# Loads, gate bias, a PSUM bank and the last tile: four edits to the order of an adaLN block

## The chip, the cores and the metric

One Trainium2 chip, one core. The number is the device time of one execution in microseconds. Three runs of the kernel before took 184.07, 186.6 and 189.16 us, median 186.6. The profiled execution took 184.51 us, of which the profile's span is 182.8; TensorE's granted clock was full throughout.

## The reference

Four batches (B = 4) of 512 tokens, hidden width H = 512, all in float32. A modulation vector per batch comes from `silu(c) @ wmod` in six sections (sa, ca, ga, sb, cb, gb). Then one block with one attention head of width 128, and a linear layer with four low-rank experts of rank 8, of which the gate picks one per token:

```python
mod = (_silu(L0_c) @ L0_wmod).reshape(L0_c.shape[0], 6, 1, -1)
ga = (2 * (ga >= 0) - 1) * jnp.maximum(jnp.abs(ga), 0.25)      # gb alike
h = _layernorm(x) * (1 + ca) + sa
x = x + ga * attention(h)        # q, k, v of width 128; softmax; Wo; bo
h = _layernorm(x) * (1 + cb) + sb
x = x + gb * (h @ W_up.T + lora_B[e] @ (lora_A[e] @ h))   # e = argmax(h @ gate_w.T + bias)
```

## The kernel before

Every product is made of three TensorE products of high and low parts (`products`, L391), so that each operand exists as `hi` and `lo`: ACT writes `hi` while it empties a PSUM bank, DVE subtracts it and writes `lo`. A batch is worked in these steps: layer norm 1 (DVE statistics, POOL's power, ACT or DVE normalises into `xn1`), `h1` = normalised x turned and scaled by `1 + ca`, `qkv`, scores `S`, maxima (DVE), softmax (ACT), probabilities turned (`PT`), `O`, out projection `Y`, residual and layer norm 2 (DVE, POOL, ACT), `h2`, gate and low-rank logits `gz`, their turning to tokens (`zl`, L587), the choice of the expert (DVE), `zT`, up projection `F` (four tiles of 128 tokens) closed by `lora_up` (L618), the gate product `f_gb` (DVE, L1280), the last sum (POOL, or DVE for the last two tiles, L1408), the store.

The five engines run programs written out by hand, in order, with semaphores. The programs of batch b interleave two batches: PE does batch b's attention between the pieces of batch b - 1's up projection, and then `qkv(b + 1)`. SP issues all DMAs from one queue.

In batches 0 and 1, `x` is turned by TensorE. In batches 2 and 3 (`TURNED`) it is turned in blocks of 32 by DVE (`turn_blocks`, L1148), and then 16 SBUF-to-SBUF copies on SP's queue put the blocks in place (`move_turned`, L318, from `xn` to `stage`). `h1_high` (ACT, L782) waits for all 16.

The eight PSUM banks are handed out by the table `psum_plan`: each use of a bank waits until the bank's earlier use was emptied (`open_bank`). In it, `m` are the five banks of the attention part and `f` three of the up projection. F(b - 1, 3) is in the bank of F(b - 1, 0), which is free once DVE has written `f_gb` of tile 0; on DVE this stands behind `h1_low(b + 1)`, the residual and the layer norm 2 statistics of batch b's tile 0.

`gz_evacuate` (ACT, L904) adds a bias per expert. For batch 0 this bias must be computed first: TensorE (`gate_shift_columns`), then DVE (`gate_shift`, L1118 and L1122), which in batch 1's pass stands behind `turn_blocks(2)` and `v_low`. `gate_columns("gb")` makes the second gate, TensorE turns it (`gate_to_rows`), DVE writes it to `gates`, and SP sends it to DRAM (`write_gate`, L299) and spreads it over the partitions from there.

At the start x of batch 0, the section ca, `Wqkv` and sa are issued one after the other. TensorE's `modulation(0)` needs ca; `qkv_shift_columns` (L454) needs the row of qkv's shift, which DVE adds up (`qkv_shift_row`, L1107) after the layer norm 1 of batch 1.

## Time and profile before

| | us |
|---|---|
| median of three runs | 186.6 (184.07 to 189.16) |
| profiled execution | 184.51 |
| its span | 182.8 |
| PE busy | 170.1, 93% of the span |
| DVE busy | 139.8, 76% |
| ACT busy | 90.3, 49% |
| POOL busy | 81.0, 44% |

Starts are counted from the beginning of the span. An engine's idle time stands in square brackets behind the instruction that ended it, with what released it. Starts of consecutive matmuls tell their pace; their own durations overlap.

### The profile page before, as it was taken

How to read it: one execution, taken by the hardware profiler on the slowest of the kernel's cores; microseconds unless marked ns; L12 is line 12 of the kernel's file. 1: busy time of each engine (PE TensorE's matmuls, PEld its weight loads, DVE VectorE, ACT ScalarE, POOL GpSimd, SP SyncE). 2: the span in 40 equal slices, each digit the busy share in tenths (PEclk: the TensorE clock that was granted, in tenths of full speed). 3: DMA queues.
4: the chain of work that ended last, by engine and by line, in shares of the span. 5: the costliest groups of instructions: out<-in, count | busy, mean ns of one | idle time of the engine just before them, and what ended most of it. 6: DMA issues, size and time to landing. Idle time of an engine off the chain costs nothing.

```text
span 182.8 us, 2810 instructions
## 1 busy us (share of the span) xinstructions
PE 170.1 (93%) x911; PEld 133.6 (73%) x911; DVE 139.8 (76%) x350; ACT 90.3 (49%) x170; POOL 81.0 (44%) x109
## 2 busy tenths in 40 slices
PE   6778999999999959998999999999999999999990
PEld 6654756978678738786888787868887878768870
DVE  1837859997969999869997919699288294988964
ACT  3356145964268874176438552713396512484100
POOL 3464200279335984008769830018695000362650
PEclk9999999999999999999999999999999999999999
DMA  4999995930051014440023741001140000001414
GB/s 155 381 385 387 390 383 98 375 120 11 0 166 69 2 26 105 102 170 6 32 83 136 190 107 31 0 0 57 61 152 24 0 2 0 0 0 61 172 43 186
DMA packets 13758, 21.32 MB, mean 117 GB/s; under 512 B 3324, under 2 KB 3840, under 8 KB 13744
## 3 DMA queue, kind: packets, MB, share of 16 engines
q1 hardware_dynamic: 13744, 21.15, 34.3%
q8 instruction: 7, 0.11, 0.3%
q14 instruction: 7, 0.06, 0.1%
HBM read 14.83 MB, written 4.21 MB: 104 GB/s over the span
## 4 chain that ended last, share of the span: by engine, by line
PE 65%; DVE 18%; ACT 6%; DMA 4%; issue 4%; SPq 1%; POOL 0%; DVEq 0%; ACTq 0%; POOLq 0%
PE bank L391 43%; DMA stage<-in_L_wmod_dram 4%; PE bank L405 3%; DVE h1lo L1137 3%; PE bank L515 3%; DVE xs L1215 2%; DVE stats L1222 2%; PE bank L542 2%; DVE row_max L1189 2%; ACT xn_p L830 2%; DVE f_gb L1280 2%; DVE h2lo L1153 1%; DVE xn L1148 1%; PE bank L494 1%; PE bank L500 1%
## 5 line engine op out<-in xcount | busy, mean ns | idle before, releaser
L391 PE MATMUL bank<-wup_lo,h2hi 128*128 128x512 f32 x64 | 26.8, 418 | 1.3 <-DVE f_gb L1280 0.9
L1466 POOL TENSOR_TENSOR rstd<-var_eps,neg_half 128x1 f32<-128x1 f32 x16 | 8.8, 553 | 41.4 <-DVE var_eps L1226 41.4
L869 ACT ACTIVATE xn_p<-xs,shift,rstd 128x512 f32<-128x512 f32 x16 | 13.1, 817 | 25.9 <-POOL shift L1469 25.9
L391 PE MATMUL bank<-wup_hi,h2hi 128*128 128x512 f32 x64 | 25.3, 395 | 0.0
L391 PE MATMUL bank<-wup_hi,h2lo 128*128 128x512 f32 x64 | 25.2, 394 | 0.0
L1481 POOL TENSOR_TENSOR xs<-xs,f_gb 128x512 f32<-128x512 f32 x14 | 17.9, 1294 | 7.7 <-DVE f_gb L1280 7.7
L391 PE MATMUL bank<-h1lo,wqkv_hi 128*128 128x512 f32 x48 | 19.7, 410 | 0.8 <-DVE modT_ca L1057 0.8
L1458 POOL TENSOR_TENSOR xs<-xs,gabo 128x512 f32<-128x512 f32 x16 | 20.2, 1293 | 0.1
L391 PE MATMUL bank<-h1hi,wqkv_hi 128*128 128x512 f32 x48 | 19.0, 395 | 0.0
L391 PE MATMUL bank<-h1hi,wqkv_lo 128*128 128x512 f32 x48 | 18.9, 394 | 0.0
L391 PEld LDWEIGHTS bank<-wup_lo,h2hi 128*128 128x128 f32 x64 | 12.0, 188 | 4.5 <-DVE f_gb L1280 1.8
L1198 DVE TENSOR_TENSOR plo<-bank,phi 128x512 fp32r<-128x512 f32 x16 | 10.0, 684 | 6.8 <-ACT phi L838 6.7
L391 PEld LDWEIGHTS bank<-wup_hi,h2hi 128*128 128x128 f32 x64 | 12.0, 188 | 2.8
L1215 DVE SCALAR_TENSOR_TENSOR xs<-bank,row_inv,xs 128x512 f32<-128x512 f32 x16 | 12.0, 748 | 2.2 <-PE bank L391 1.3
L391 PEld LDWEIGHTS bank<-wup_hi,h2lo 128*128 128x128 f32 x64 | 12.1, 189 | 2.0
L830 ACT ACTIVATE xn_p<-bank,neg_max 128x512 f32<-128x512 f32 x16 | 11.0, 687 | 4.9 <-DVE neg_max L1191 4.9
L1003 DVE BATCH_NORM_STATS2 stats<-xs 128x6 f32<-128x512 f32 x16 | 10.2, 679 | 3.4 <-DMA xs<-in_L_attn_x_dram 3.4
L391 PEld LDWEIGHTS bank<-h1lo,wqkv_hi 128*128 128x128 f32 x48 | 9.0, 188 | 4.2 <-issue 2.4
L1443 POOL TENSOR_TENSOR wo_ga<-wo_raw,ga_bc 128x512 f32<-128x512 f32 x4 | 5.6, 1396 | 14.1 <-DMA ga_bc<-gates_dram 10.9
L1280 DVE TENSOR_TENSOR f_gb<-bank,gb_bc 128x512 f32<-128x512 f32 x16 | 10.6, 687 | 1.6 <-PE bank L618 1.5
L1222 DVE BATCH_NORM_STATS2 stats<-xs 128x6 f32<-128x512 f32 x16 | 11.1, 695 | 0.8
L838 ACT ACTIVATE phi<-bank 128x512 fp32r<-128x512 f32 x16 | 8.4, 606 | 6.0 <-PE bank L515 6.0
(181 smaller groups left out, 414.5 us busy)
## 6 DMA issues: line engine op xcount, KB each, us to landing
out_dram<-xs SPq DMA_DIRECT2D x16, 256.0 KB, 2.0
...
xs<-in_L_wmod_dram SPq DMA_DIRECT2D x3, 1024.0 KB, 10.1
...
stage<-xn SPq DMA_DIRECT2D x32, 64.0 KB, 2.0
...
gb_bc<-gates_dram SPq DMA_DIRECT2D x4, 256.0 KB, 3.7
```

Source lines behind the costliest of these rows:

```text
L391: mm = nc.tensor.matmul(dst, w, m, start=first and i == 0, stop=last and i == total - 1)
L830: nc.scalar.activation(xn2_p[:, t, :], at("S", b, t)[:], ACT.Exp, bias=neg_max[:, t:t + 1], scale=SCORE_SCALE, accum_out=row_sum[:, t:t + ...
L838: nc.scalar.activation(phi[:, :, t * P:(t + 1) * P], at("PT", b, t)[:].rearrange("p (k q) -> p k q", k=NT), ACT.Copy).then_inc(S["pt_hi"], 1)
L869: nc.scalar.activation(xn2_p[:, t, :], xs[:, b, t, :], ACT.Identity, bias=shift[:, 1, t:t + 1], scale=rstd[:, 1, t:t + 1]).then_inc(S["xn2 ...
L1003: nc.vector.bn_stats(stats[:, 0, t, :], xs[:, b, t, :]).then_inc(S["ln1_stats"], 1)
L1198: nc.vector.tensor_tensor(plo[:, :, q], at("PT", b, t)[:].rearrange("p (k q) -> p k q", k=NT), phi[:, :, q].bitcast(F32), ALU.subtract).th ...
L1215: nc.vector.scalar_tensor_tensor(xs[:, b, t, :], at("Y", b, t)[:], row_inv[:, t:t + 1], xs[:, b, t, :], ALU.mult, ALU.add).then_inc(S["x2_ ...
L1222: nc.vector.bn_stats(stats[:, 1, t, :], xs[:, b, t, :]).then_inc(S["ln2_stats"], 1)
L1280: nc.vector.tensor_tensor(f_gb[:, n % 4, :], at("F", b, t)[:], gb_bc[:, b % 2, :], ALU.mult).then_inc(S["f_gb_ready"], 1)
L1458: nc.gpsimd.tensor_tensor(xs[:, b, t, :], xs[:, b, t, :], gabo[:], ALU.add).then_inc(S["xb_ready"], 1)
L1466: nc.gpsimd.tensor_tensor(rstd[:, 1, t:t + 1], var_eps[:, 1, t:t + 1], neg_half[:, 0:1], ALU.pow).then_inc(S["ln2_rstd"], 1)
L1481: nc.gpsimd.tensor_tensor(xs[:, b, t, :], xs[:, b, t, :], f_gb[:, n % 4, :], ALU.add).then_inc(S["out_ready"], 1)
```

## The change

Four things are edited.

1. **Loads.** x of batch 0 comes in three loads (tile 0, tile 1, tiles 2 and 3). SP issues the first half of `Wqkv` only when tile 1 is in, and section sa only when all of x is in. DVE normalises tile 3 of x before it writes the first modulation rows, and TensorE turns tile 3 before the modulation columns.
2. **Gate bias.** In batch 1's pass, DVE does `gate_shift` and `gate_columns("gb")` right behind the maxima, `turn_blocks(2)` behind `v_low`, and the statistics of batch 3 behind `o_low`. ACT does `wo_high(1)` and two of the four normalisations of batch 2 after `gz_evacuate(0)`. SP puts the write of the second gate between the first eight and the last eight copies of turned blocks.
3. **Bank.** F(b - 1, 3) of batches 0 and 1 is in the bank of zT(b - 1), and qkv(b + 1)'s first output in the bank of F(b - 1, 0).
4. **Last tile.** The last tile of the last batch is computed in two halves of 256 columns, each in a bank of its own, with a multiply, an add and a store of its own, and `z_transposes` of the second half stands before it.

```diff
@@ -77,15 +77,15 @@
...
         order += [(m[4], "zT", b - 1), (f[2], "F", b - 1, 2)]
-        order += [(m[i], "Y", b, t) for t, i in enumerate((1, 2, 3, 0))] + [(f[0], "F", b - 1, 3)]
+        order += [(m[i], "Y", b, t) for t, i in enumerate((1, 2, 3, 0))] + [(f[0] if last else m[4], "F", b - 1, 3)]
         if not last:
-            order += [(m[i], "qkv", b + 1, j) for j, i in enumerate((4, 1, 2))]
+            order += [(f[0], "qkv", b + 1, 0), (m[1], "qkv", b + 1, 1), (m[2], "qkv", b + 1, 2)]
             order += [(m[3], "x2T", b, 0), (m[0], "x2T", b, 1), (f[1], "x2T", b, 2), (f[2], "x2T", b, 3)]
-            m, f = (f[0], m[4], m[1], m[2], m[3]), (m[0], f[1], f[2])
+            m, f = (m[4], f[0], m[1], m[2], m[3]), (m[0], f[1], f[2])
         else:
...
                       (m[0], "x2T", b, 3), (m[1], "gz", b, 0), (m[4], "F", b, 1), (m[3], "zl", b, 0), (m[1], "gz", b, 1),
-                      (f[0], "zl", b, 1), (f[1], "F", b, 2), (m[0], "zT", b, 0), (f[2], "F", b, 3), (m[1], "zT", b, 1)]
+                      (f[0], "zl", b, 1), (f[1], "F", b, 2), (m[0], "zT", b, 0), (m[1], "zT", b, 1), (f[2], "side", 0), (m[3], "side", 1)]
     place, earlier, holds = {}, {}, [None] * 8
...
@@ -196,7 +196,7 @@
...
         wqkv_in = [sem(f"wqkv_in{kt}") for kt in range(NK)]
-        x0_in = [sem(f"x0_in{i}") for i in range(2)]
+        x0_in = [sem(f"x0_in{i}") for i in range(3)]
         x_in = [sem(f"x_in{b}") for b in range(B)]
...
@@ -264,6 +264,9 @@
...
 
+        def columns_of(side):
+            return slice(side * H // 2, (side + 1) * H // 2)
+
         def xn1_done(engine, b, t=NT):
...
@@ -297,9 +300,9 @@
...
                 sp.dma_start(gates_dram[i], gates[:, i, :]).then_inc(gates_out, 16)
+
+            def spread_gate(i, b):
                 sp.wait_ge(gates_out, 16 * (i + 1))
-
-            def spread_gate(i, b):
                 if b >= 2 and i == 0:
...
@@ -308,22 +311,25 @@
...
 
-            def move_turned(b):
-
-                sp.wait_ge(S["xn1_turned"], NT * (b - TURNED + 1))
-                if b > TURNED:
-                    sp.wait_ge(S["h1_lo"], NK * b)
-                for a in range(NB):
+            def move_turned(b, blocks=range(NB)):
+
+                if blocks[0] == 0:
+                    sp.wait_ge(S["xn1_turned"], NT * (b - TURNED + 1))
+                    if b > TURNED:
+                        sp.wait_ge(S["h1_lo"], NK * b)
+                for a in blocks:
                     for c in range(NB):
...
             sp.dma_start(c_rows[0:B, :], c).then_inc(c_in, 16)
-            for i in range(2):
-                sp.dma_start(xs[:, 0, 2 * i:2 * i + 2], x_v[0, :, 2 * i:2 * i + 2, :]).then_inc(x0_in[i], 16)
+            for i, ts in enumerate((slice(0, 1), slice(1, 2), slice(2, 4))):
+                sp.dma_start(xs[:, 0, ts], x_v[0, :, ts, :]).then_inc(x0_in[i], 16)
             load_section("ca")
+            sp.wait_ge(x0_in[1], 16)
             load_wqkv((0, 1))
+            sp.wait_ge(x0_in[2], 16)
             load_section("sa")
...
@@ -351,8 +357,9 @@
...
             sp.dma_start(xs[:, 3], x_v[3]).then_inc(x_in[3], 16)
-            move_turned(2)
+            move_turned(2, (0, 1))
             write_gate(1)
+            move_turned(2, (2, 3))
             spread_gate(1, 0)
...
@@ -360,15 +367,17 @@
...
                     move_turned(3)
-                for t in range(NT):
-                    if b == LAST and t >= 2:
-                        sp.wait_ge(last_out_ready, t - 1)
-                    else:
-                        sp.wait_ge(S["out_ready"], NT * b + t + 1)
+                for t in range(NT if b < LAST else 2):
+                    sp.wait_ge(S["out_ready"], NT * b + t + 1)
                     sp.dma_start(out_v[b, :, t, :], xs[:, b, t, :]).then_inc(stored, 16)
...
                     spread_gate(1, b + 2)
-            sp.wait_ge(stored, 16 * B * NT)
+            sp.wait_ge(last_out_ready, 1)
+            sp.dma_start(out_v[LAST, :, 2, :], xs[:, LAST, 2, :]).then_inc(stored, 16)
+            for side in range(2):
+                sp.wait_ge(last_out_ready, 2 + side)
+                sp.dma_start(out_v[LAST, :, 3, columns_of(side)], xs[:, LAST, 3, columns_of(side)]).then_inc(stored, 16)
+            sp.wait_ge(stored, 16 * (B * NT + 1))
 
...
@@ -618,6 +627,16 @@
...
 
+            def last_tile_side(side, kts):
+
+                q, n = slice((NT - 1) * P, T), columns_of(side)
+                whole = open_bank("side", side) if kts[0] == 0 else at("side", side)
+                dst = whole[:, n]
+                products(dst, [((h2hi[:, kt, q], h2lo[:, kt, q]), (wup_hi[:, kt, n], wup_lo[:, kt, n])) for kt in kts],
+                         first=kts[0] == 0, last=False)
+                if kts[-1] == NK - 1:
+                    nc.tensor.matmul(dst, zT[:, q], lbw[:, n], start=False, stop=True).then_inc(S["F_psum"], 1)
+
             def gate_transposes():
...
@@ -679,9 +698,9 @@
...
             first_x1_transposes((2,))
+            first_x1_transposes((3,))
             first_modulation_columns(0)
             first_modulation_columns(1)
-            first_x1_transposes((3,))
             keep_warm(bank[5], 3)
...
@@ -764,12 +783,12 @@
...
             lora_up(b, 1)
-            up(b, 3, (0, 1))
             z_transposes(b, 1)
-            up(b, 3, (2,))
+            for side in range(2):
+                last_tile_side(side, (0, 1, 2))
             lora_up(b, 2)
-            up(b, 3, (3,))
-            lora_up(b, 3)
+            for side in range(2):
+                last_tile_side(side, (3,))
 
...
@@ -845,8 +864,8 @@
...
 
-            def ln1_normalise(b):
-                for t in range(NT):
+            def ln1_normalise(b, tiles=range(NT)):
+                for t in tiles:
                     act.wait_ge(S["ln1_shift"], BY_ACT + NT * (b - 2) + t + 1)
...
@@ -955,14 +974,16 @@
...
             h2_high(0)
-            wo_high(1)
-            ln1_normalise(2)
+            ln1_normalise(2, (0, 1))
             for b in range(1, B):
...
                 gz_evacuate(b - 1)
+                if b == 1:
+                    wo_high(1)
+                    ln1_normalise(2, (2, 3))
                 pt_high(b)
...
@@ -996,7 +1017,7 @@
...
                     if b == 0:
-                        dve.wait_ge(x0_in[t // 2], 16)
+                        dve.wait_ge(x0_in[min(t, 2)], 16)
                     else:
...
@@ -1310,8 +1331,8 @@
...
                 first_ln1_variance(t)
+            first_ln1_normalise()
             first_modulation_rows()
-            first_ln1_normalise()
             first_columns(0)
...
@@ -1357,14 +1378,11 @@
...
                 if b == 1:
-                    turn_blocks(2)
+                    gate_shift()
+                    gate_columns("gb")
                 v_low(b)
                 if b == 1:
-                    gate_shift()
-                    ln1_stats(3, (0, 1, 2, 3))
-                    ln1_moments(3)
-                if b == 1:
-                    gate_columns("gb")
+                    turn_blocks(2)
                 pt_low(b)
...
@@ -1372,6 +1390,8 @@
...
                 if b == 1:
+                    ln1_stats(3, (0, 1, 2, 3))
+                    ln1_moments(3)
                     ffn_shift_rows()
...
@@ -1401,11 +1421,20 @@
...
             gate_ffn(LAST, 1)
-            for t in (2, 3):
-                gate_ffn(LAST, t)
-                n = NT * LAST + t
-                dve.wait_ge(S["f_gb_ready"], n + 1)
-                nc.vector.tensor_tensor(xs[:, LAST, t, :], xs[:, LAST, t, :], f_gb[:, n % 4, :],
+            gate_ffn(LAST, 2)
+            n = NT * B - 2
+            dve.wait_ge(S["f_gb_ready"], n + 1)
+            nc.vector.tensor_tensor(xs[:, LAST, 2, :], xs[:, LAST, 2, :], f_gb[:, n % 4, :],
+                                    ALU.add).then_inc(last_out_ready, 1)
+            n = NT * B - 1
+            dve.wait_ge(S["out_ready"], n - 3)
+            for side in range(2):
+                part = columns_of(side)
+                dve.wait_ge(S["F_psum"], n + side + 1)
+                nc.vector.tensor_tensor(f_gb[:, n % 4, part], at("side", side)[:, part], gb_bc[:, LAST % 2, part],
+                                        ALU.mult).then_inc(S["f_gb_ready"], 1)
+                dve.wait_ge(S["f_gb_ready"], n + side + 1)
+                nc.vector.tensor_tensor(xs[:, LAST, 3, part], xs[:, LAST, 3, part], f_gb[:, n % 4, part],
                                         ALU.add).then_inc(last_out_ready, 1)
...
```

**DVE, batch 1's pass, behind the scores.** Before, behind the last `neg_max`; `gz_sum` and `gz_bias` the gate bias, `stats<-xs` the statistics of batch 3:

```order
L1148 STREAM_TRANSPOSE xn<-xn 128x16x32 x4
L1182 TENSOR_TENSOR v_lo<-bank,v_hi 128x512
L1118 TENSOR_REDUCE gz_sum<-bank 72x4
L1122 TENSOR_SCALAR gz_bias<-gz_sum,eb_col 72x4
L1003 BN_STATS stats<-xs 128x6 x4
L1008 BN_AGGR moments<-stats 128x2 x4
L1010 TENSOR_SCALAR var_eps<-moments 128x4
L1088 SCALAR_TENSOR_TENSOR gate_tmp<-mod_sum 128x16
L1090 TENSOR_SCALAR gate_tmp<-mod_sum 128x16
L1093 TENSOR_SCALAR gate_tmp<-gate_tmp 128x16
L1096 SCALAR_TENSOR_TENSOR gate_col<-gate_tmp 128x16
L1198 TENSOR_TENSOR plo<-bank,phi 128x4x128 x4
```

Now:

```order
L1212 TENSOR_SCALAR neg_max<-row_max 128x1
L1139 TENSOR_REDUCE gz_sum<-bank 72x4
L1143 TENSOR_SCALAR gz_bias<-gz_sum,eb_col 72x4
L1109 SCALAR_TENSOR_TENSOR gate_tmp<-mod_sum 128x16
L1111 TENSOR_SCALAR gate_tmp<-mod_sum 128x16
L1114 TENSOR_SCALAR gate_tmp<-gate_tmp 128x16
L1117 SCALAR_TENSOR_TENSOR gate_col<-gate_tmp 128x16
L1203 TENSOR_TENSOR v_lo<-bank,v_hi 128x512
L1169 STREAM_TRANSPOSE xn<-xn 128x16x32 x4
L1219 TENSOR_TENSOR plo<-bank,phi 128x4x128 x4
L1123 COPY gates<-bank 4x512
```

The bias and the second gate moved ahead of `v_lo`, the block turns behind it, and the statistics out of the piece.

**ACT, the same place.** Before; `xn_p,row_sum` is the softmax, `xn<-xs` the normalisation of batch 2:

```order
L880 ACTIVATE h2hi<-bank,modT_cb 128x512 x4
L895 ACTIVATE wo_hi<-wo_ga 128x512
L856 ACTIVATE xn<-xs,shift,rstd 128x4x4x32 x4
L830 ACTIVATE xn_p,row_sum<-bank,neg_max 128x512 x3
L819 ACTIVATE v_hi<-bank 128x512
L830 ACTIVATE xn_p,row_sum<-bank,neg_max 128x512
L904 ACTIVATE gz<-bank,gz_bias 72x512
L838 ACTIVATE phi<-bank 128x4x128 x4
```

Now:

```order
L899 ACTIVATE h2hi<-bank,modT_cb 128x512 x4
L875 ACTIVATE xn<-xs,shift,rstd 128x4x4x32 x2
L849 ACTIVATE xn_p,row_sum<-bank,neg_max 128x512 x3
L838 ACTIVATE v_hi<-bank 128x512
L849 ACTIVATE xn_p,row_sum<-bank,neg_max 128x512
L923 ACTIVATE gz<-bank,gz_bias 72x512
L914 ACTIVATE wo_hi<-wo_ga 128x512
L875 ACTIVATE xn<-xs,shift,rstd 128x4x4x32 x2
L857 ACTIVATE phi<-bank 128x4x128 x4
```

`wo_hi` and two of the four normalisations stand behind `gz`, the softmax comes two normalisations and a `wo_hi` sooner.

**SP, the copies of turned blocks and what follows.** Before:

```order
L353 DMA xs<-in_L_attn_x_dram 128x4x512
L318 DMA stage<-xn 32x512 x16
L299 DMA gates_dram<-gates 4x512
L309 DMA gb_bc<-gates_dram 128x512 x2
L309 DMA ga_bc<-gates_dram 128x512
L368 DMA out_dram<-xs 128x512 x4
```

Now:

```order
L359 DMA xs<-in_L_attn_x_dram 128x4x512
L322 DMA stage<-xn 32x512 x8
L302 DMA gates_dram<-gates 4x512
L322 DMA stage<-xn 32x512 x8
L312 DMA gb_bc<-gates_dram 128x512 x2
L312 DMA ga_bc<-gates_dram 128x512
L372 DMA out_dram<-xs 128x512 x4
```

The write of the gates stands between two groups of eight copies; the spreads of both gates stay behind all of them.

## Rows read from the trace of the kernel before

**Rows 1.** The page: busy time by engine; transfer rate in 40 slices of 4.6 us.
```profile
PE 170.1 (93%) x911; PEld 133.6 (73%) x911; DVE 139.8 (76%) x350; ACT 90.3 (49%) x170; POOL 81.0 (44%) x109
...
GB/s 155 381 385 387 390 383 98 375 120 11 0 166 69 2 26 105 102 170 6 32 83 136 190 107 31 0 0 57 61 152 24 0 2 0 0 0 61 172 43 186
```

**Rows 2.** Timeline of PE (start us, us, engine, line, tiles, idle before, releaser).
```profile
68.76 0.44 PE L587 MATMUL bank<-ident,gz 72*128 72x72 f32 x4 [2.27 <-ACT gz L904]
...
86.11 0.50 PE L391 MATMUL bank<-wup_lo,h2hi 128*128 128x512 f32 x1 [0.58 <-DVE f_gb L1280]
...
122.16 0.50 PE L391 MATMUL bank<-wup_lo,h2hi 128*128 128x512 f32 x1 [0.34 <-DVE f_gb L1280]
```

**Rows 3.** Chain of waits, in order of time (start us, us, what).
```profile
2.19 7.96 DMA stage<-in_L_wmod_dram
...
89.40 8.36 PE bank L391 x36
```

**Rows 4.** Timeline of DVE and PE, 17 to 25 us.
```profile
17.69 2.47 DVE L1003 BATCH_NORM_STATS2 stats<-xs 128x6 f32<-128x512 f32 x4 [0.35 <-DMA xs<-in_L_attn_x_dram]
...
23.83 0.56 DVE L1107 TENSOR_TENSOR qb_row<-bank,bqkv_rows 128x384 f32<-128x384 f32 x1
...
24.53 0.52 PE L454 MATMUL bank<-ident,qb_row 128*128 128x128 f32 x3
```

**Rows 5.** View of tile xs, batch 1's x load, issued at 5.8.
```profile
DMA to landing us min/median/max: 11.9/11.9/11.9
```

**Rows 6.** Timeline of ACT and DVE, 60 to 68 us.
```profile
60.88 2.92 ACT L856 ACTIVATE xn<-xs,shift,rstd 128x512 f32<-128x512 f32 x4
...
63.81 0.15 DVE L1191 TENSOR_SCALAR neg_max<-row_max 128x1 f32<-128x1 f32 x1
...
67.11 0.72 DVE L1122 TENSOR_SCALAR gz_bias<-gz_sum,eb_col 72x4 f32<-72x4 f32 x1
```

**Rows 7.** Timeline of ACT, DVE and PE, 79 to 108 us.
```profile
79.97 2.55 ACT L782 ACTIVATE h1hi<-stage,modT_ca 128x512 fp32r<-128x512 f32 x4
...
85.36 0.69 DVE L1280 TENSOR_TENSOR f_gb<-bank,gb_bc 128x512 f32<-128x512 f32 x1
...
93.16 2.48 DVE L1148 STREAM_TRANSPOSE xn<-xn 128x512 f32<-128x512 f32 x4
...
97.13 1.13 DVE L1172 SCALAR_TENSOR_TENSOR qk_lo<-bank,qb,qk_hi 128x128 fp32r<-128x128 f32 x4 [1.49 <-ACT qk_hi L808]
...
99.10 2.73 DVE L1153 SCALAR_TENSOR_TENSOR h2lo<-bank,modT_cb,h2hi 128x512 fp32r<-128x512 f32 x4 [0.19 <-ACT h2hi L880]
...
106.04 0.69 ACT L904 ACTIVATE gz<-bank,gz_bias 72x512 f32<-72x512 f32 x1
...
107.19 0.41 PE L587 MATMUL bank<-ident,gz 72*128 72x72 f32 x4
```

**Rows 8.** Timeline of SP's issues, 66 to 77 us.
```profile
66.39 10.10 SPq L318 DMA_DIRECT2D stage<-xn  x16
...
76.54 0.48 SPq L299 DMA_DIRECT2D gates_dram<-gates  x1
```

**Rows 9.** The page, DMA issues (count, KB each, us to landing).
```profile
out_dram<-xs SPq DMA_DIRECT2D x16, 256.0 KB, 2.0
...
stage<-xn SPq DMA_DIRECT2D x32, 64.0 KB, 2.0
```

**Rows 10.** Timeline, operations of 256 columns, and DVE's last add.
```profile
11.33 0.76 DVE L1049 TENSOR_SCALAR gb_bc<-bank 128x256 f32<-128x256 f32 x2 [1.89 <-PE bank L405]
...
169.00 0.28 PE L578 MATMUL bank<-h2hi,gzw 128*72 128x256 f32 x1
...
169.12 0.28 PE L579 MATMUL bank<-h2lo,gzw 128*72 128x256 f32 x1
...
179.61 0.69 DVE L1408 TENSOR_TENSOR xs<-xs,f_gb 128x512 f32<-128x512 f32 x1
```

**Rows 11.** The page, costliest groups (busy us, mean ns, idle before).
```profile
L391 PEld LDWEIGHTS bank<-wup_hi,h2hi 128*128 128x128 f32 x64 | 12.0, 188 | 2.8
```

## The prediction, before the changed kernel ran

> **What bounds the kernel now.** I read the page first, then the chain of waits, then the timeline around each idle stretch of PE. TensorE is busy 93% of the span [rows 1], so only time in which it stands still, and the two ends of the kernel, can be given back. Behind the start its larger stops are three [rows 2]: 2.27 us before batch 0's expert logits are turned (L587), and 0.58 and 0.34 us before the fourth up projection of batches 0 and 1, which finds its bank still held by the first. The start hangs on `ca`: issued at 2.19, in 7.96 us later, at 10.15 [rows 3]. Around it the loads run at 381 to 390 GB/s [rows 1]. The tail is DVE's multiply and add of the last tile, then a store.
>
> **Part 1, loads held back.** The bytes ahead of `ca`'s last one (x 1.05 MB, `ca` 1.05 MB) take 5.4 us at 390 GB/s, and they flow from about 2.8, so `ca` could be in at 8.2 plus the time to be reported, against 10.15: at most some 1.3 us are lost to loads behind it. The nearest evidence on whether they are: the queue was never empty, and x of batch 1, issued behind everything, landed 11.9 us after its issue [rows 5]. That is time in a full queue, not the transfer's own. [...]
>
> More important is who uses such a gain. If PE starts qkv earlier it arrives earlier at L454, the turning of the shift row. That row comes from DVE, at 23.83 + 0.56 = 24.39, and PE takes it at 24.53 [rows 4]. DVE's work between runs without a break of note from x of batch 1, which DVE waited for until 17.69 (ln1 statistics, POOL's power, four normalisations, the shift row) [rows 4]. PE's slack there is 0.1 us. So whatever `ca` gains is handed back at L454 unless x of batch 1 also lands earlier, and that load moves behind two waits. Moving the modulation rows behind tile 3's normalisation, and PE's columns behind tile 3's transposes, costs at most the 0.2 us of four transposes, and is absorbed at the same place. Bounds -1.3 and +2.4 (the latter below, as a rival); I take **0**, since the row nearest to it, L454, has no slack.
>
> **Part 2, gate bias ahead.** PE's 2.27 us wait ends with ACT's `gz`, and this with DVE's `gz_bias`, which starts at 67.11 [rows 6] behind four block turns and v_low. Now it stands right behind the last negated maximum (63.96), so it is ready at about 64.9. ACT no longer normalises four tiles first (2.92 us from 60.88 [rows 6]); two of them and wo_high come behind `gz`. Its softmaxes then follow DVE's maxima, and `gz` is done at about 65.7, before PE needs it at 66.3. The whole stop goes: **-2.27** on PE. The work put aside must still be done. ACT after 63.96: softmax, `gz` and wo_high at 0.7 each (a `gz` takes 0.69 [rows 7]), two normalisations at 0.73: about 67.6. DVE's last of four turns, 0.62 of 2.48 [rows 7], ends near 68.4, where all four ended at 66.39 before. pt_low starts there, in time for pv at 71.6. Statistics of batch 3 (2.5 us) move behind o_low into a stretch in which DVE then waits for ACT's h1; I cost them at nothing, and if that cover went, 2.5 us would fall on h1_low.
>
> The copies of turned blocks do not hide. The 16 issues take 10.10 us on SP [rows 8], the last lands 2.0 us after its issue [rows 9]. They start 2.0 later, and between the eighth and the ninth stands the write of the gates, 0.48 us [rows 8] (its data is there at 72.2, before the eighth issue ends). The last copy was in at 77.9 and now is at 80.4. ACT began batch 2's h1 at 79.97 [rows 7], so h1 and all that DVE has queued behind it come **0.5 later** than before, while PE is 2.27 earlier.
>
> **Part 3, the bank.** F(0,3) now follows zT(0), which is emptied 6 us earlier, so the 0.58 disappears where it stood; PE could be at the end of up(0,3) at 89.40 - 2.27 - 0.58 = 86.55 (89.40 is where qkv(2) began [rows 3]). But qkv(2) has now the bank of F(0,0), so the wait for the same evacuation moves there: 85.36 + 0.69 [rows 7] + 0.5 = 86.55. By luck the two meet; qkv(2) starts about 2.8 earlier.
>
> **Where part of it is given back.** Scores of batch 2 need qk_lo. DVE's second set of turns ended at 93.16 + 2.48 = 95.64 and qk_lo started at 97.13, having waited for ACT, which waited for PE [rows 7]. With PE 2.8 earlier and DVE 0.5 later, qk_lo is bound by DVE's queue: it starts at 96.2, only 0.95 earlier. h2_low, which stood behind it with a small wait (0.19), comes 1.1 earlier, and so do the maxima and softmaxes. ACT's `gz` moves from 106.04 to 104.95 and ends at 105.65; PE, which was at L587 at 107.19 [rows 7] without a wait, waits now until then. Left: **-1.55**. In batch 2 the bank change takes 0.34 away [rows 2]; there h1 waited for PE and not for copies, so nothing is late: **-0.34**. From there all engines keep step with PE.
>
> **Part 4, the last tile in halves.** 24 matmuls of 256 columns stand for 12 of 512. The nearest rows, logits in halves, follow each other at 0.12 us [rows 10], 24 of them as long as 12 at 0.23: 0. If each instead took the 188 ns of a full weight load [rows 11], PE would be 24 x 0.07 = 1.7 later. I take 0, since in the rows with 256 columns the load was hidden. DVE then does two multiplies and two adds of half size. A half-size operation took 0.38 (0.76 for two), a whole one 0.69 [rows 10], so four against two are 0.14 more, partly overlapped: **+0.1**. DVE was the last to finish (179.61 + 0.69). The last store has half the bytes, but 64 KB copies and 256 KB stores both land in 2.0 [rows 9]: 0. The end gains nothing, which is the opposite of what the edit suggests.
>
> **Sum:** 0 - 1.55 - 0.34 + 0.1 = -1.8 us. The profiled execution took 184.51 (span 182.8), which gives 182.7. The three runs are 184.07, 186.6 and 189.16; with the profiled one their median is 1.05 above it. I add that much: **183.7**.
>
> **Rivals.**
> - *The start pays too (B).* x of batch 1 lands earlier with `ca`, and the 1.3 us pass L454: 181.4. For it: `ca` was 1.3 us later than its bytes. Against it: queue full before and after, L454 without slack.
> - *The copies eat it (C).* SP takes the gate write late, or batch 3's copies, which start half a microsecond later too, hold ACT, or the statistics put off push h1_low: 1 to 2 us more for DVE's queue behind 80.4, and every microsecond of it goes through qk_lo to PE: about 184. For it: 10.10 us of issues for one pass. Against it: DVE has 2 us of idle time before h1_low.
> - *Slower (D): the held loads come late.* x of batch 1 was issued at 5.8 and is now issued behind two waits, at about 8.2. Should its 11.9 us from issue to landing [rows 5] be its own time, it lands 2.4 later, at 20.1, and DVE's chain from 17.69 to 24.39 moves by 2.4, with PE at L454 behind it. Slower than before from a delay of 1.8 us on; at 2.4: 182.7 + 2.4 = 185.1. Against it: full bandwidth until then [rows 1], so its bytes should not be later.
> - *The bank change does nothing*: partly in the forecast already, since in batch 1 the wait only moves from up(0,3) to qkv(2); it costs or saves 0.6 at most.
>
> **Chances.** Forecast 0.52, B 0.23, C 0.15, D 0.10. The forecast's own range is 1.2 to 2.9 us of gain. Over the cases the sums reach from 181.4 to 185.1; the medians of runs can lie from 0.6 below to 1.9 above such a sum: 180.8 to 187.0. A measurement of this kernel can tell about 2%, 3.7 us. The forecast is 1% and B 1.7%; only with halves of B, or all bounds on the good side, or runs of before that all fall high, is it over 2% faster: 0.27. Slower by over 2% takes D and more: 0.06. Within: 0.67.
>
> **What would show it.** L587 of batch 0 without idle time, at about 66.3. SP's first copies at 68.4, the gate write between eight and eight, ACT's first `h1hi<-stage` at 80.4 rather than 79.97. No wait of PE before up(0,3); one for `f_gb` before qkv(2), or none. qk_lo of batch 2 straight behind the block turns, and a short wait of PE at scores and at L587 of batch 1. `ca` at 9 to 10 and PE at L454 still at 24.4 to 24.6: if it is at 23.2, B is right; at 26 or later, D. At the end, DVE's last add 0.1 later behind PE's last matmul than before. The forecast is wrong if the start moves L454, if a weight load shows between the half-size matmuls, or if copies take longer than 10.1 us to issue.

## The result and the profile after

| | before | after |
|---|---|---|
| median of 11 runs, us | 184.51 (183.73 to 189.21) | 182.92 (181.78 to 183.54) |
| profiled execution | 184.51 | 182.96 |
| its span | 182.8 | 181.2 |
| PE busy | 170.1 (93%) | 170.8 (94%) |

The ratio is 0.9923, 95% interval 0.9894 to 0.9951: faster by 0.8%, less than the 2% called a difference. Runs of the kernel before (and, below, of e10) fall in two groups, here six around 184 (median 184.03) and four around 189, with one at 186.6 between them, of which the ratios use the lower one alone; none of the changed kernel's runs lay near 189.

First the page of the changed kernel, to be held against [rows 1]; slices of 4.53 us.

```profile
PE 170.8 (94%) x924; PEld 134.9 (74%) x924; DVE 139.6 (77%) x352; ACT 90.1 (50%) x170; POOL 80.4 (44%) x109
...
GB/s 130 313 352 379 387 385 234 269 206 52 0 54 183 0 0 50 98 109 157 0 114 33 213 139 83 0 0 56 65 149 26 0 2 0 0 4 58 174 41 190
```

The loads are slower at the start: over the first four slices 1174 GB/s summed against 1308 before, which over 4.55 us each is 0.61 MB not yet moved. Profiles of the experiments below bear this out: the four kernels in which SP waits between loads have sums of 1174 to 1266, the ten others 1268 to 1320.

Timeline of PE: its stops from 8 us on that a bracket names, and four places without one (lines are shifted: L596 is L587 of before, L463 is L454, L400 is L391). Two more stops are not shown, since the kernel before has them too: 0.26 us at 38.27 (before 0.26 at 37.48) and 0.38 at 161.53 (before 0.37 at 163.00).

```profile
10.59 1.07 PE L414 MATMUL bank<-stage,silu_wide 128*32 128x512 f32 x8 [2.24 <-DMA stage<-in_L_wmod_dram]
15.61 0.47 PE L400 MATMUL bank<-h1lo,wqkv_hi 128*128 128x512 f32 x1 [1.17 <-ACT wqkv_hi L881]
25.32 0.52 PE L463 MATMUL bank<-ident,qb_row 128*128 128x128 f32 x3
...
67.12 0.41 PE L596 MATMUL bank<-ident,gz 72*128 72x72 f32 x4
87.54 0.47 PE L400 MATMUL bank<-h1lo,wqkv_hi 128*128 128x512 f32 x1 [0.40 <-DVE f_gb L1301]
98.69 0.50 PE L509 MATMUL bank<-qk_lo,qk_hi 128*128 128x512 f32 x1 [0.15 <-DVE qk_lo L1197]
106.31 0.44 PE L596 MATMUL bank<-ident,gz 72*128 72x72 f32 x4
...
132.21 1.91 PE L551 MATMUL bank<-ident,xn_p 128*128 128x128 f32 x16
```

Of the stops in [rows 2] none is left where it stood. In exchange there are 0.40 us before batch 2's qkv and 0.15 before its scores, and the start is late: L454 was reached at 24.53 [rows 4], now at 25.32.

Timeline of DVE, ACT and SP, the pieces that answer to [rows 4], [rows 6], [rows 7] and [rows 8].

```profile
18.41 2.47 DVE L1024 BATCH_NORM_STATS2 stats<-xs 128x6 f32<-128x512 f32 x4 [0.39 <-DMA xs<-in_L_attn_x_dram]
...
24.62 0.56 DVE L1128 TENSOR_TENSOR qb_row<-bank,bqkv_rows 128x384 f32<-128x384 f32 x1 [0.21 <-PE bank L455]
...
64.89 0.23 DVE L1143 TENSOR_SCALAR gz_bias<-gz_sum,eb_col 72x4 f32<-72x4 f32 x1
65.86 0.68 ACT L923 ACTIVATE gz<-bank,gz_bias 72x512 f32<-72x512 f32 x1
...
69.24 5.04 SPq L322 DMA_DIRECT2D stage<-xn  x8
74.33 0.48 SPq L302 DMA_DIRECT2D gates_dram<-gates  x1
74.85 4.94 SPq L322 DMA_DIRECT2D stage<-xn  x8
...
81.30 2.56 ACT L801 ACTIVATE h1hi<-stage,modT_ca 128x512 fp32r<-128x512 f32 x4 [2.88 <-DMA stage<-xn]
86.70 0.69 DVE L1301 TENSOR_TENSOR f_gb<-bank,gb_bc 128x512 f32<-128x512 f32 x1
94.49 2.48 DVE L1169 STREAM_TRANSPOSE xn<-xn 128x512 f32<-128x512 f32 x4
96.90 1.08 DVE L1193 SCALAR_TENSOR_TENSOR qk_lo<-bank,qb,qk_hi 128x128 fp32r<-128x128 f32 x4
```

`gz_bias` starts at 64.89, `gz` at 65.86, and PE finds it done at 67.12. Then the new chain. The view of the chain of waits of the changed kernel, 67 to 87 us, shows it (start, us, what):

```profile
67.80 1.43 DVE xn L1169 x2
69.24 0.61 SPq L322
...
79.20 2.02 DMA stage<-xn
81.30 0.73 ACT h1hi L801
82.05 1.90 DVE h1lo L1158 x3
```

The program's end now goes through SP: block turns, seventeen issues one behind the other, the landing of the last copy, h1, DVE's queue, and from there to PE. On the page, SP's issues are 6% of the chain that ended last, and were 1% before.

### The profile page after: what moved, and what is told of

The parts are those of the page before. It is cut to its first block, busy times and chain, and to the rows that moved or that the text cites. A ratio compares the mean times of both kernels' runs of the same rounds, so it can differ in the third digit from the quotient of the medians.

```text
span 181.2 us, 2841 instructions
## 1 busy us (share of the span) xinstructions
PE 170.8 (94%) x924; PEld 134.9 (74%) x924; DVE 139.6 (77%) x352; ACT 90.1 (50%) x170; POOL 80.4 (44%) x109
## 4 chain that ended last, share of the span: by engine, by line
PE 57%; DVE 18%; ACT 8%; SPq 6%; DMA 6%; issue 4%; POOL 0%; DVEq 0%; ACTq 0%; POOLq 0%
PE bank L400 37%; SPq L322 5%; DMA stage<-in_L_wmod_dram 4%; PE bank L414 3%; DVE xs L1236 3%; ACT xn_p L849 3%; DVE stats L1243 3%; DVE xn L1169 2%; PE bank L524 2%; DVE f_gb L1301 1%; DVE h1lo L1158 1%; DVE h2lo L1174 1%; PE bank L509 1%; PE bank L503 1%; DMA stage<-xn 1%
## 5 line engine op out<-in xcount | busy, mean ns | idle before, releaser
L400 PE MATMUL bank<-wup_lo,h2hi 128*128 128x512 f32 (+1 forms) x68 | 27.2, 401 | 0.4 <-ACT h2hi L907 0.4
L400 PE MATMUL bank<-wup_hi,h2hi 128*128 128x512 f32 (+1 forms) x68 | 26.0, 382 | 0.0
L400 PE MATMUL bank<-wup_hi,h2lo 128*128 128x512 f32 (+1 forms) x68 | 25.9, 381 | 0.0
L400 PE MATMUL bank<-h1lo,wqkv_hi 128*128 128x512 f32 x48 | 19.7, 411 | 1.6 <-ACT wqkv_hi L881 1.2
L1487 POOL TENSOR_TENSOR xs<-xs,gabo 128x512 f32<-128x512 f32 x16 | 20.3, 1308 | 0.1
L400 PE MATMUL bank<-h1hi,wqkv_hi 128*128 128x512 f32 x48 | 19.0, 395 | 0.0
L400 PE MATMUL bank<-h1hi,wqkv_lo 128*128 128x512 f32 x48 | 18.9, 394 | 0.0
L400 PEld LDWEIGHTS bank<-wup_lo,h2hi 128*128 128x128 f32 x68 | 12.8, 188 | 2.7 <-issue 0.6
L400 PEld LDWEIGHTS bank<-wup_hi,h2hi 128*128 128x128 f32 x68 | 12.8, 188 | 2.6
L400 PEld LDWEIGHTS bank<-wup_hi,h2lo 128*128 128x128 f32 x68 | 12.9, 189 | 1.9
L400 PEld LDWEIGHTS bank<-h1lo,wqkv_hi 128*128 128x128 f32 x48 | 9.0, 188 | 5.4 <-issue 2.3
L1301 DVE TENSOR_TENSOR f_gb<-bank,gb_bc 128x512 f32<-128x512 f32 x15 | 9.9, 685 | 1.7 <-PE bank L627 1.5
L1210 DVE TENSOR_REDUCE row_max<-bank 128x1 f32<-128x512 f32 x16 | 10.9, 681 | 0.1
L400 PEld LDWEIGHTS bank<-h1hi,wqkv_hi 128*128 128x128 f32 x48 | 9.0, 188 | 2.2
```

Source lines behind the costliest of these rows:

```text
L400: mm = nc.tensor.matmul(dst, w, m, start=first and i == 0, stop=last and i == total - 1)
L1210: nc.vector.reduce_max(row_max[:, t:t + 1], at("S", b, t)[:], AX_X).then_inc(S["max_ready"], 1)
L1301: nc.vector.tensor_tensor(f_gb[:, n % 4, :], at("F", b, t)[:], gb_bc[:, b % 2, :], ALU.mult).then_inc(S["f_gb_ready"], 1)
L1487: nc.gpsimd.tensor_tensor(xs[:, b, t, :], xs[:, b, t, :], gabo[:], ALU.add).then_inc(S["xb_ready"], 1)
```

## The experiments

Unless a time is called a span, it is a median of runs. Spans are those of the profiled executions; ratios are to runs of the kernel before on the same chip. The experiments ran in three groups, each on a chip of its own: e1, e2, e3 and e5; e6 to e9; e4, e10, e11 and e12. Medians are compared safely within a group only; across groups the ratios are to be compared, with their intervals. "Old start" means part 1 undone.

**e1: part 1 undone, everything else as changed.**

```diff
-            for i, ts in enumerate((slice(0, 1), slice(1, 2), slice(2, 4))):
-                sp.dma_start(xs[:, 0, ts], x_v[0, :, ts, :]).then_inc(x0_in[i], 16)
+            for i in range(2):
+                sp.dma_start(xs[:, 0, 2 * i:2 * i + 2], x_v[0, :, 2 * i:2 * i + 2, :]).then_inc(x0_in[i], 16)
             load_section("ca")
-            sp.wait_ge(x0_in[1], 16)
             load_wqkv((0, 1))
-            sp.wait_ge(x0_in[2], 16)
...
-            first_ln1_normalise()
             first_modulation_rows()
+            first_ln1_normalise()
```

> The changed kernel with its start as before: x in two loads, nothing held back, the modulation rows and columns in their old order. The other three parts stay. My theory (the held loads cost time): in the changed kernel ca is in at 10.55 instead of 10.15 and PE is at L454's turning at 25.45 instead of 24.53, so undoing the start gives 0.9 us back: ca at 10.15, L454 at 24.5, the first turned logits about 65.5, qkv(2) at 86.7, span 180.3, ratio to the kernel before 0.987. Rival (the difference at the start is spread between executions of one and the same program, or is swallowed later where DVE and SP bind): the span stays at 181.2, ratio 0.992.

Measured: 182.16 (181.69 to 182.78), ratio 0.9886 [0.9853, 0.9919], span 180.3. Timeline of DVE and PE of e1:

```profile
16.87 2.46 DVE L1022 BATCH_NORM_STATS2 stats<-xs 128x6 f32<-128x512 f32 x4
...
24.26 0.52 PE L461 MATMUL bank<-ident,qb_row 128*128 128x128 f32 x3
```

DVE takes x of batch 1 at 16.87, not 18.41, and PE is at the shift row 1.06 us before the changed kernel. The span is shorter by 0.9 us. The intervals of the two ratios overlap, so e1 alone does not prove that part 1 costs; e10, and e11 against e12, do. Which piece of it costs, the next four ask.

**e2, e3, e4, e10: the pieces of part 1.** e2 keeps the three loads and the new order and drops SP's two waits. e3 keeps the waits and the order, with x in two loads. e4 keeps the order alone. e10 is the kernel before with part 1 alone.

```diff
 e2, against the changed kernel
-            sp.wait_ge(x0_in[1], 16)
...
-            sp.wait_ge(x0_in[2], 16)
 e3, against the changed kernel
-            for i, ts in enumerate((slice(0, 1), slice(1, 2), slice(2, 4))):
+            for i in range(2):
...
-            sp.wait_ge(x0_in[1], 16)
+            sp.wait_ge(x0_in[0], 16)
             load_wqkv((0, 1))
-            sp.wait_ge(x0_in[2], 16)
+            sp.wait_ge(x0_in[1], 16)
```

> The changed kernel without the two waits in SP's queue: x still in three loads, new order on DVE and PE. If the waits starve the transfer engines (313 GB/s in the second fortieth of the span against 381 before), this one has 380 there, all of x in by 6.3, ca at 10.2 to 10.5 (its issue stays 0.4 later), L454 at 24.6 to 24.9. If the smaller first loads are what slows the transfers, the rate stays near 313, all of x is in at 7.9 and L454 stays at 25.4.

> The changed kernel with x in two loads as before, but with the waits: the first half of Wqkv is issued when the first half of x is in, section sa when all of it is. If the waits starve the transfers: rate near 313 in the second fortieth, second half of x later than 6.1, ca at 10.2 or later, L454 near 25.1. If the split in three is the cause: rate 380, ca earlier than 10.15, L454 at 24.5.

> The changed kernel with the loads of before (two loads of x, no waits on SP's queue), but the new order on DVE (tile 3 normalised before the first modulation rows) and on TensorE (tile 3 turned before the modulation columns). Theory: the order alone costs at most 0.3 us, since the work only changes places ahead of the same landing of x of batch 1; PE at L454 at 24.2 to 24.6, time as with the whole start of before, 182.2. Rival: the order is what costs, 0.5 us or more, PE at L454 at 24.9 or later with x of batch 1 landing at 17.5 or before.

> The kernel before with part 1 alone: x of batch 0 in three loads, the two waits on SP's queue, and the new order of DVE and TensorE at the start. Theory (the start costs, because held loads arrive later): PE reaches the turning of the shift row (L454) at 25.1 to 25.4 instead of 24.1 to 24.6, x of batch 1 lands at about 18.4, and since the rest is the order of before, with its 2.27 us stop at L587 that waits for ACT and DVE, which are late by the same 0.8, all of it passes on: 0.7 to 0.9 us slower than before, span about 183.6. Rival (the start is neutral, and the 0.8 us between the changed kernel and the one with the old start was the spread between executions): no difference, ratio 1.000. Rival of the prediction (start pays): 1 us faster.

Starts in the profiled executions (us), and medians:

| | x loads | waits | order | `ca` issued | PE takes `ca` | to qkv(0) | DVE takes x of batch 1 | L454 | median | ratio |
|---|---|---|---|---|---|---|---|---|---|---|
| before | 2 | no | old | 2.19 | 10.20 | +4.62 | 17.69 | 24.53 | 184.51 | 1 |
| e8 | 2 | no | old | 2.19 | 10.30 | +4.62 | 17.81 | 24.63 | | |
| e1 | 2 | no | old | 2.19 | 9.32 | +5.23 | 16.87 | 24.26 | 182.16 | 0.9886 [0.9853, 0.9919] |
| e4 | 2 | no | new | 2.19 | 9.46 | +5.03 | 17.01 | 24.20 | 182.09 | 0.9888 [0.9867, 0.9909] |
| e2 | 3 | no | new | 2.57 | 9.99 | +5.03 | 17.51 | 24.73 | 182.49 | 0.9895 [0.9865, 0.9925] |
| e3 | 2 | yes | new | 2.19 | 10.39 | +5.02 | 17.87 | 25.12 | 181.96 | 0.9863 [0.9816, 0.9911] |
| after | 3 | yes | new | 2.57 | 10.59 | +5.02 | 18.41 | 25.32 | 182.92 | 0.9923 [0.9894, 0.9951] |
| e11 | 3 | yes | new | 2.56 | 10.17 | +5.03 | 18.64 | 25.26 | 181.59 | (another edit, below) |

The ratios of e1 to e4 can't be told apart: their intervals overlap, and e3, with the waits, has the lowest. So the medians don't say which piece costs, and what follows on the pieces is read from starts in single profiles.

e10, part 1 alone on the kernel before, has the ratio 1.0044 [1.0022, 1.0067]: 0.8 us slower. Its interval leaves out no change, and gain as well. It rests on three of its nine runs (184.68 to 185.25), and the median of all nine is 190.3. In its profiled execution, span 190.7, TensorE's clock fell behind `ca` (last section), so it is not in the table.

One regularity reads the table: in twelve of the thirteen profiles with the clock at full level there, PE reaches L454 9.70 to 9.72 us after it starts qkv(0). No bracket names a wait on the way, so what is late at qkv(0) is late at L454. Only in e11 does it wait there, 0.22 us for DVE's row, behind the latest x of batch 1, at 18.64. So DVE's row and PE run nearly level, and elsewhere PE's own work sets when it arrives.

From before to after that gives +0.39 for `ca` and +0.40 for what lies between `ca` and qkv(0). In this pair of traces the first is an issue: the third load of x puts `ca` on the queue at 2.57 instead of 2.19, and it lands in 7.98 us against 7.96. From one profile to the next the landing varies more than that, from 6.8 to 8.1 us without waits, so the pair can't show it by itself. The second is the order. Timeline of PE of e9 (old order, described below), then of e4 (new order), which both take `ca` at the same time:

```profile
9.44 1.07 PE L412 MATMUL bank<-stage,silu_wide 128*32 128x512 f32 x8 [0.59 <-DMA stage<-in_L_wmod_dram]
...
11.16 0.60 PE L469 MATMUL bank<-ident,xn 128*128 128x128 f32 x4
11.59 0.60 PE L420 MATMUL bank<-ident,gb_bc 128*128 128x128 f32 x4
...
14.26 0.47 PE L398 MATMUL bank<-h1lo,wqkv_hi 128*128 128x512 f32 x1 [0.77 <-ACT wqkv_hi L879]
```

```profile
9.46 1.06 PE L412 MATMUL bank<-stage,silu_wide 128*32 128x512 f32 x8 [0.48 <-DMA stage<-in_L_wmod_dram]
...
11.17 1.04 PE L469 MATMUL bank<-ident,xn 128*128 128x128 f32 x8
12.05 0.60 PE L420 MATMUL bank<-ident,gb_bc 128*128 128x128 f32 x4
...
14.49 0.47 PE L398 MATMUL bank<-h1lo,wqkv_hi 128*128 128x512 f32 x1 [1.17 <-ACT wqkv_hi L879]
```

Tile 3's four transposes (L469, eight in a row instead of four) take 0.44 us ahead of the columns (L420), and the columns make `modT_ca`, without which no h1 is. With `ca` at 9.45 this costs 0.2 at qkv(0), where the old order is not bound by the columns: tile 3's transposes then wait for DVE to normalise it (in e1, with `ca` at 9.32, PE waits 0.41 us for that, and the distance is even +5.23). With `ca` later than 9.8 the old order's distance is 4.62 to 4.65 in five profiles and the new one's 5.02, the whole 0.4. e4's median does not show it.

Last the waits. SP's issues of e1 and of the changed kernel tell what they do. First e1:

```profile
2.70 0.99 SPq L294 DMA_DIRECT2D xn_p<-in_L_attn_Wqkv_dram  x2
...
5.66 0.38 SPq L335 DMA_DIRECT2D xs<-in_L_attn_x_dram  x1
```

and the changed kernel:

```profile
4.55 1.07 SPq L294 DMA_DIRECT2D xn_p<-in_L_attn_Wqkv_dram  x2
...
9.72 0.41 SPq L337 DMA_DIRECT2D xs<-in_L_attn_x_dram  x1
```

x of batch 1 (L337) is issued 4.06 us later than in e1 and used 1.54 later: most of its time was queue, but not all. And `ca`, for which the others stood back, gained nothing: PE took it at 10.17 to 10.84 in the four profiles with waits (e10's included), at 9.05 to 10.30 in the ten without, and from issue to landing it took 7.6 to 8.2 us with waits, 6.8 to 8.1 without. That the waits make it later is likely but not shown, since those ranges overlap and e3's median is no worse than e1's; that they don't bring it forward is.

**e5: the last tile whole, old start.**

```diff
-            for side in range(2):
-                last_tile_side(side, (0, 1, 2))
+            up(b, 3, (0, 1))
+            z_transposes(b, 1)
+            up(b, 3, (2,))
             lora_up(b, 2)
-            for side in range(2):
-                last_tile_side(side, (3,))
+            up(b, 3, (3,))
+            lora_up(b, 3)
```

> Start as before and the last tile whole as before; gate bias and bank as in the changed kernel. In the changed kernel DVE's last add ended 0.27 us later behind the gate product of tile 2 than before (3.01 against 2.74), but the span ended 2.1 us behind that add against 2.5. My theory: the halves cost DVE 0.27 and the half-size store gives 0.4 back, so this kernel is 0.1 us slower than e1_old_start, not to be told apart by its time; from the tile-2 gate product to the end of the span 5.2 us here, 5.1 in e1. Rival (as forecast: the store gives nothing): 0.1 to 0.3 us faster than e1_old_start.

Measured: 182.13 (181.75 to 182.31), ratio 0.9882 [0.9861, 0.9903], span 180.5; e1 182.16. Timeline of DVE at the end, e1 first, then e5:

```profile
175.15 0.69 DVE L1299 TENSOR_TENSOR f_gb<-bank,gb_bc 128x512 f32<-128x512 f32 x1 [1.54 <-PE bank L625]
...
177.73 0.42 DVE L1435 TENSOR_TENSOR xs<-xs,f_gb 128x256 f32<-128x256 f32 x1
```

```profile
175.28 0.69 DVE L1297 TENSOR_TENSOR f_gb<-bank,gb_bc 128x512 f32<-128x512 f32 x1 [1.52 <-PE bank L623]
...
177.33 0.69 DVE L1424 TENSOR_TENSOR xs<-xs,f_gb 128x512 f32<-128x512 f32 x1
```

From tile 2's product to the last add's end it is 3.00 us with halves and 2.74 whole; from there to the span's end 2.15 and 2.48. DVE loses 0.26, and 0.33 comes back behind its last add, where the last store has half the size. Part 4 is worth nothing either way.

**e6: the gate write behind all sixteen copies, old start.**

```diff
-            move_turned(2, (0, 1))
-            write_gate(1)
-            move_turned(2, (2, 3))
+            move_turned(2)
+            write_gate(1)
```

> Start as before; gate bias, bank and halves as in the changed kernel, but SP writes the second gate behind all 16 copies instead of between eight and eight. If the issue of the copies is what binds batch 2's h1 (ACT started it at 80.31 in e1_old_start, released by the last copy), the last copy and h1 come 0.5 earlier (79.8), the gate product of tile 0 too (85.2), and qkv(2) starts at 86.1 instead of 86.55; 0.4 us less in the span: 179.9. The gate spreads land about 1 us later, which I expect to be hidden. Rival (POOL's output weights, which wait for the spread, bind layer norm 2): h1 0.5 earlier, but nothing gained or up to 0.5 lost by the scores of batch 2.

Measured: 182.85 (181.88 to 183.34), ratio 0.9868 [0.976, 0.9976], span 181.3: not the gain of 0.4 that was expected. The copies took 10.34 us instead of 10.52 with the write between them (e1), and ACT's h1 began 11.86 us behind their start instead of 12.06. Against these 0.2 us the spreads of the gates started 1.5 later on SP (80.32 against 78.83), since they wait for the write to land. The way from there to PE can be read in the two traces: POOL, which multiplies the output weights by the spread gate (`wo_ga`), starts that at 86.35 instead of 84.80, POOL's powers for layer norm 2 stand behind it in its queue, and ACT's first `xn_p` of batch 1's layer norm 2, which needs them, starts at 89.80 instead of 88.25. ACT's last is late too, and PE stops where e1 had no stop. Timeline of PE of e6:

```profile
95.79 1.97 PE L548 MATMUL bank<-ident,xn_p 128*128 128x128 f32 x16 [0.75 <-ACT xn_p L885]
```

By these traces the place of the write is right: between the copies it costs 0.2 us, behind them some 0.8 us of span (1.0, of which 0.2 stood already at L454, 24.44 against 24.26). The ratios of e6 and e1 don't tell them apart.

**e7: the bank table as before, all other parts but the start changed. e8: the kernel before with the new bank table alone.**

```diff
 e7, against the changed kernel (besides the old start)
-        order += [...] + [(f[0] if last else m[4], "F", b - 1, 3)]
+        order += [...] + [(f[0], "F", b - 1, 3)]
...
-            m, f = (m[4], f[0], m[1], m[2], m[3]), (m[0], f[1], f[2])
+            m, f = (f[0], m[4], m[1], m[2], m[3]), (m[0], f[1], f[2])
 e8, against the kernel before: the same lines the other way round
```

> Start as before, gate bias and halves as in the changed kernel, the bank plan as before: F(0,3) again behind F(0,0). My theory: the two parts are worth something only together, because the DVE queue is 0.3 to 0.5 later and PE waits there: up(0,3) starts only at 86.5 with 3.5 us of idle time before it, qkv(2) at 89.8, scores at 99.9, in batch 2 another 0.4; the span 182.8 to 183.3, no better than the kernel before, ratio 0.997 to 1.003. Rival (the gains add up one by one): 1.0 to 1.3 us slower than e1_old_start, span 181.5, ratio 0.994.

> The kernel before with the new bank plan alone. My theory: here the DVE queue keeps its old times, qkv(2) may start at once behind up(0,3), so both stops go: 0.7 in batch 1's pass and 0.5 in batch 2's, span 181.6, ratio 0.9935. Rival (the wait only moves to qkv(2), which now shares the bank of F(0,0)): qkv(2) where it was at 89.3, span 182.3 or more, ratio 0.998.

e7: 186.07 (184.63 to 187.54; 186.00 over the five runs that the ratio uses), ratio 1.0032 [0.9937, 1.0128], span 184.4. e8: 184.95 (182.55 to 187.3; 183.93 over the four that the ratio uses), ratio 0.9932 [0.9792, 1.0072], span 181.5. Timeline of PE of e7, the fourth up projection of batch 0 and what follows:

```profile
82.52 0.40 PE L625 MATMUL bank<-lbw,zT 128*128 128x512 f32 x1
86.23 0.65 PE L398 MATMUL bank<-wup_lo,h2hi 128*128 128x512 f32 x1 [3.31 <-DVE f_gb L1299]
...
87.11 0.63 PE L398 MATMUL bank<-wup_hi,h2hi 128*128 128x512 f32 x1
87.54 0.63 PE L398 MATMUL bank<-wup_lo,h2hi 128*128 128x512 f32 x1
...
90.22 0.39 PE L398 MATMUL bank<-wup_hi,h2lo 128*128 128x512 f32 x1
90.46 0.39 PE L398 MATMUL bank<-wup_hi,h2hi 128*128 128x512 f32 x1
```

and PE's busy time by windows there (window, length, busy, granted clock, DMA share, GB/s):

```profile
86.00:88.00 2.00, 1.77 (x5) 0.61 0.00 0
88.00:90.00 2.00, 2.00 (x7) 0.54 0.00 0
90.00:92.00 2.00, 2.00 (x10) 1.00 0.34 131
```

Without the new bank the time that PE gains at L587 is lost in front of the fourth up projection, which finds its bank held until DVE's `f_gb` at 85.49: the stop there grows from 0.58 to 3.31 us. Behind it the granted clock is at its lower level, 1.2 GHz: eight matmuls follow each other at 0.42 to 0.43 us instead of 0.235, another 1.5 us. qkv(2) starts at 90.92, 4.4 us after e1's 86.55. The one run of e7 with a mean granted clock of 1.0 took 184.63, the four others that the ratio uses, at 0.986 to 0.991, 185.92 to 186.2. In its trace part 2 without the bank is a loss: batch 1's L587 comes at 108.93, later than the 107.19 of [rows 7]; by the ratio it is no gain. The bank alone (e8) is a gain of its own by its trace, 1.3 us of span, while its ratio's interval also holds no change: its stop at L587 is 2.27 as before, but L587 of batch 1 comes at 106.55 and batch 2's x turns, at 133.66 before, at 132.41. Together (e1) they come at 105.33 and 131.21. The parts don't add: e7 has 1.6 us more span than the kernel before, e8 1.3 less, and e1 with both 2.5 less.

**e9: ACT issues four of batch 2's sixteen copies, old start; e12 the same kernel on another chip; e11 the same edit on the changed kernel with its own start.**

```diff
             move_turned(2, (0, 1))
             write_gate(1)
-            move_turned(2, (2, 3))
+            move_turned(2, (2,))
...
                 pt_high(b)
+                if b == 1:
+                    act.wait_ge(S["xn1_turned"], NT)
+                    for c in range(NB):
+                        nc.scalar.dma_start(turned_x1[3 * BLOCK:4 * BLOCK, c].rearrange("p k e -> p (k e)"),
+                                            xn1_blocks[c * BLOCK:(c + 1) * BLOCK, 3].rearrange("p k t i -> p (k t i)")
+                                            ).then_inc(turned_moved, 16)
                 o_high(b)
```

> As e1_old_start, but four of batch 2's sixteen copies are issued by ACT behind pt_high, where ACT is idle for almost 4 us, so SP issues 12. If SP's issue time is what gives part of the gain back, the last copy lands about 2.5 us earlier, ACT starts h1 at 78.0 to 78.5, the waits before qkv(2) (0.56), scores (0.31) and the turned logits (0.16) go, and the span is 179.3, ratio 0.982. Rival (the copies are bound by the transfer engines, or DVE's own work binds behind them): h1 starts at 80 or the span stays within 0.3 of 180.3.

> The same kernel as the one with the old start in which ACT issues four of the sixteen copies of batch 2, run again as the yardstick of this group and as a second measurement of the fastest version: 180.5 us within 0.5, span 178.5 within 0.5, PE at L454 between 23.9 and 24.6.

> The changed kernel, its new start included, with the last four of batch 2's sixteen copies of turned blocks issued by ACT behind the evacuation of the turned probabilities' high parts, instead of by SP. Theory: start cost and copy queue are separate, one delays every engine and the other only h1 of batch 2, so the split gains what it gained with the old start, 1.8 us of span (179.4 here), and the distance of 0.8 us to the kernel with the old start and the same split stays. Rival: one hides in the other, the distance is 0.3 or less.

| | median | ratio | span | h1 of batch 2 | L587 of batch 1 |
|---|---|---|---|---|---|
| e9 | 180.51 | 0.9757 [0.9681, 0.9832] | 178.5 | 77.78 | 103.62 |
| e12 | 180.38 | 0.9810 [0.9787, 0.9834] | 178.6 | 77.82 | 103.62 |
| e11 | 181.59 | 0.9876 [0.9829, 0.9922] | 179.8 | 79.19 | 104.90 |

Timeline of ACT of e9, with its own queue (ACTq):

```profile
69.32 1.97 ACTq L989 DMA_DIRECT2D stage<-xn  x3
73.99 0.60 ACT L863 ACTIVATE o_hi<-bank 128x512 fp32r<-128x512 f32 x1 [4.52 <-PE bank L398]
...
77.78 2.57 ACT L799 ACTIVATE h1hi<-stage,modT_ca 128x512 fp32r<-128x512 f32 x4 [0.72 <-DMA stage<-xn]
```

ACT had nothing to do there: it waits 4.52 us for PE before `o_hi`. The last copy is in and h1 begins 2.53 us before e1's 80.31. SP's first copy went out 0.40 earlier too (67.85 against 68.25), so the four issues are worth 2.13; in e11 against the changed kernel it is 2.02 by the same count (h1 10.04 us behind the first copy instead of 12.06). In e9 PE has no stop that a bracket names between 66 and 110 us, and the span is 1.8 shorter than e1's, of which 0.3 stood at L454 (23.97 against 24.26); e11's is 1.4 shorter than the changed kernel's. This is the fastest version: 180.4 to 180.5, by e12's ratio 1.9% under the kernel before. The Trainium skill (DMA: Bandwidth & Descriptors, "Issuing engines are not separate DMA queues") says that issuing from several engines saves only the sequencer's time, "usually small relative to the DMA itself". Here that time was not small: one issue behind the other, sixteen copies took 10.10 us, while each landed 2.0 after its issue [rows 8, 9], and it lay on the path.

e11 against e12 gives the start's cost again, free of the copies: 1.2 us (180.38 against 181.59). The intervals of the two ratios leave room for the 0.8 of e10 as well.

## Why the prediction was right, and where it was wrong

The number held: 183.7 forecast, 182.92 measured; from the profiled execution 182.7 against 182.96. That the sum held to 0.2 us is partly luck, since an error in one step offset errors in others. By starts of the same work in the two traces:

| step | forecast | measured |
|---|---|---|
| part 1 (PE at L454) | 0 | 25.32 - 24.53 = +0.79 |
| parts 2 and 3, to L587 of batch 1 | -1.55 | -0.88 - 0.79 = -1.67 |
| batch 2, to the x turns | -0.34 | -1.45 + 0.88 = -0.57 |
| behind that, tail in halves | +0.1 | -1.6 + 1.45 = -0.15 |
| span | -1.8 | -1.6 |

**Part 1 was wrong**: the prediction put it at 0 and it cost 0.8 us, in two small terms and one large view. "`ca` could be in" earlier failed first: held-back loads did not shorten its landing in any of four profiles (7.6 to 8.2 us, against 6.8 to 8.1). But one issue more, 0.38 us, stood ahead of it, which the prediction did not count. The second term, "costs at most the 0.2 us of four transposes, and is absorbed at the same place", was 0.44 for the transposes and nothing was absorbed. And the place was misread: DVE's row ends 0.14 us before PE comes to L454 since it waits for PE's own products (L455, 0.21 in the changed kernel), so the row follows PE. Where it does lead, in e11, it ends 6.47 us after DVE takes x of batch 1; before it took 6.70, so DVE had 0.2 us to spare. "The forecast is wrong if the start moves L454", says the prediction, and for this part that came true. Rival D's delay of x of batch 1 came too, 0.72 instead of 2.4, alongside and hidden but for e11's bracket of 0.22.

**Part 2 was right in its mechanism**, the stop gone and `gz_bias` right behind the last negated maximum. It was ready at 65.12 for the forecast 64.9, although the start was 0.79 late, since it took 0.23 us instead of 0.72. The worth of the part was 2.42, not 2.27: before, PE's last matmul started at 66.10, the next could have at 66.34, and came at 68.76. A bracket is counted from a modelled end and leaves out some 0.15 us; the three stops of [rows 2] held 0.45 more than their brackets, which covers the 0.35 that the sum to L587 and batch 2 gained beyond the forecast.

**Copies and the bank were right in their mechanism.** With the old start (e1) ACT's h1 began at 80.31 (forecast 80.4), after the block turns, eight issues, the write and eight more; qkv(2) at 86.55 (forecast 86.55), with a wait for `f_gb` there and none before the fourth up projection; L587 of batch 1 at 105.33 for 105.65. Of the two sums that met at 86.55, DVE's was the right one. PE's was too late by 0.46: it took 89.40, a row of the chain, for the start of qkv(2), whose first matmul stood at 89.24, and the two stops by their brackets. That the saving at L587 is given back through DVE's queue was named in its place (qk_lo straight behind the block turns, 96.90 in the changed kernel, a short wait before scores), and the copies issued by ACT show the cause by removing it: in e11, with the start of the changed kernel, h1 2.11 earlier and L587 1.41 earlier. What the prediction did not say is that parts 2 and 3 need each other: it called the bank change "0.6 at most", and the spans of e7 and e1 are 4.1 us apart (184.4 and 180.3), of which 1.5 by the clock. Even alone, in e8's trace, the bank took 1.3 us off the span.

**Part 4 was right**: no weight load shows between matmuls of 256 columns (they follow each other at 0.12 us), and DVE's end is 0.26 later, not 0.14. That the half store gives nothing was off by 0.33, and the two cancel.

**The median.** The 1.05 us added for the distance of the profiled execution to the median of three was a mistake of reading: of three runs 5 us apart, the middle one is no typical run. The changed kernel's median lies on its profiled execution.
